# Attention with 1024-column steps, two exponentials a step, row maxima laid down by DMA, and the output's two parts added by a transfer in the projection

## The reference: what is computed

```python
ada = silu(c) @ W_ada + b_ada
h = _modulate(_layernorm(x), shift_msa, scale_msa)
qkv = (h @ W_qkv + b_qkv).reshape(b, l, 3, H, D)      # H = 16 heads of D = 36, l = 1024
scores = einsum('blhd,bmhd->bhlm', q * D ** -0.5, k)
attn = softmax(scores, axis=-1)
o = einsum('bhlm,bmhd->blhd', attn, v).reshape(b, l, c)
x = x + gate_msa * (o @ W_proj + b_proj)
# then an MLP of width 4 * 576 with its gate, and x + (z @ R - z) @ U^T
```

## Time and profile before

| | us |
|---|---|
| device time, median of 3 (3438.27 to 3440.93) | 3439.12 |
| span of the profiled execution, first to last instruction | 3409.0 |
| time outside the span (the difference) | 30.1 |
| attention, first score tile to last store | 760 to 2013 |
| projection, its stage | 2015 to about 2305 |
| busy in the span: TensorE, VectorE, ScalarE, GpSimd | 2925.1, 1807.5, 1467.3, 1632.2 |

### The profile page before, as it was taken

How to read it: one execution, slowest core, us unless ns; L and a number is a source line. 1 busy time by engine, 2 the same in 40 slices (tenths; PEclk the granted TensorE clock), 3 DMA queues, 4 the chain that set the end, 5 groups by cost and what they waited for, 6 DMA issues and landing times. The chain is left out here.

```text
span 3409.0 us, 53673 instructions
## 1 busy us (share of the span) xinstructions
PE 2925.1 (86%) x16130; PEld 2355.6 (69%) x16130; DVE 1807.5 (53%) x3056; ACT 1467.3 (43%) x2832; POOL 1632.2 (48%) x1401
## 2 busy tenths in 40 slices
PE   6759889968888898888889867757999999999976
PEld 2247677745656665665656536656999999999975
DVE  3445465447888888888888857770111111111125
ACT  2122222217888888888888852221111111111112
POOL 1232222116888888888888866781222222222210
PEclk9769899978999999999999978878999999999989
DMA  5379999983323332333323234659211112121144
GB/s 175 118 239 178 182 226 187 167 170 67 67 67 74 67 75 64 73 68 69 71 65 77 64 105 168 238 180 326 67 34 59 42 34 67 34 67 34 42 118 161
DMA packets 457636, 373.83 MB, mean 110 GB/s; under 512 B 293649, under 2 KB 357785, under 8 KB 457486
## 3 DMA queue, kind: packets, MB, share of 16 engines
q1 hardware_dynamic: 450008, 359.12, 42.1%
q10 hardware_dynamic: 7482, 12.69, 1.2%
HBM read 221.81 MB, written 149.36 MB: 109 GB/s over the span
## 5 line engine op out<-in xcount | busy, mean ns | idle before, releaser
L755 POOL TENSOR_TENSOR a_pl<-a_pf,a_ph 128x512 fp32r<-128x512 f32 x768 | 1040.3, 1386 | 215.7 <-ACT a_ph L830 215.2
L770 DVE TENSOR_REDUCE a_mx<-a_psum_s 128x1 f32<-128x1024 f32 x512 | 618.7, 1219 | 178.6 <-PE a_psum_s L861 173.9
L830 ACT ACTIVATE a_ph<-a_pf 128x512 fp32r<-128x512 f32 x1024 | 673.1, 657 | 0.0
L825 ACT ACTIVATE a_pf<-a_psum_t 128x512 f32<-128x512 f32 x1024 | 634.6, 620 | 57.0 <-PE a_psum_t L878 54.3
L1434 POOL TENSOR_TENSOR m_al<-m_af,m_ah 128x256 fp32r<-128x256 f32 x288 | 213.0, 740 | 767.9 <-DVE m_ah L1443 767.9
L1482 PE MATMUL m_psum_h<-m_ht,m_w 128*128 128x256 f32 x4032 | 534.1, 284 | 34.9 <-DMA m_w<-w_s 24.4
L1482 PEld LDWEIGHTS m_psum_h<-m_ht,m_w 128*128 128x128 f32 x4032 | 508.4, 189 | 38.3 <-issue 37.0
L1443 DVE CAST m_ah<-m_af 128x256 fp32r<-128x256 f32 x288 | 84.5, 293 | 840.6 <-ACT m_af L1420 840.6
L1496 PE MATMUL m_psum_y<-m_w,m_ah 128*128 128x288 f32 x2304 | 505.9, 296 | 1.4 <-DVE m_y L1460 1.2
L1420 ACT ACTIVATE m_af<-m_psum_h,m_bias 128x256 f32<-128x256 f32 x288 | 137.0, 476 | 817.9 <-PE m_psum_h L1482 817.9
L893 PE MATMUL a_psum_o<-a_ph,a_vs 128*100 128x512 f32 x1024 | 438.2, 428 | 32.5 <-DVE a_pl L803 25.6
(11 more groups left out here) (218 smaller groups left out, 3111.0 us busy)
## 6 DMA issues: line engine op xcount, KB each, us to landing
a_qs<-q_s SPq DMA_DIRECT2D x192, 144.0 KB
a_ks<-k_s SPq DMA_DIRECT2D x192, 144.0 KB
w_s<-q_ws SPq DMA_DIRECT2D x64, 324.0 KB, 3.8
h_s<-p_ht SPq DMA_DIRECT2D x40, 512.0 KB, 5.1
m_ht<-h_s SPq DMA_DIRECT2D x16, 1280.0 KB, 8.4
v_s<-q_vo SPq DMA_DIRECT2D x64, 288.0 KB, 8.7
a_vs<-v_s SPq DMA_DIRECT2D x128, 144.0 KB
q_s<-q_qko SPq DMA_DIRECT2D x32, 512.0 KB, 3.7
```

Source lines behind the costliest of these rows:

```text
L755: pool.tensor_tensor(pl[:, s % RING], pf[:, s % RING], raw(ph[:, s % RING]), ALU.subtract).then_inc(lo_pool, 1)
L770: dve.tensor_reduce(mx[:, u % 2, t:t + 1], p_s[:, bank(u, t)], AX.X, ALU.max) \
L825: act.activation(pf[:, s % RING], p_t[:, s % 2], ACT.Exp, scale=SCALE) \
L830: act.activation(ph[:, s % RING], pf[:, s % RING], ACT.Copy).then_inc(hi_ready, 1)
```

## The change

In the attention a step has 128 keys twice (`PAIR`), so 8 steps of 1024 columns a head; scores run 2 steps ahead. ScalarE takes the exponential twice from PSUM, once rounded to `ph` and once in full. On steps 0 and 4 (`DVE_LO`) the full one is written over the scores in PSUM, and VectorE subtracts from there; on the other six it goes to `pf`, and GpSimd subtracts. `p_t` now needs four PSUM banks, so `p_s` is a single buffer. A score tile takes every eighth query (`t:L:KT`), so that partition c of `mx` holds the maxima of 8 neighbouring queries; VectorE splits `mx` itself in two operations of 8 columns (`split_max`), and the DMA lays them down as a row. Transpose, `turn_hi` and the identity are gone. `finish` only copies 100 rows; both parts go to `o_t`, and in the projection GpSimd adds the second part onto `ot` by accumulating DMAs (`add_low`), for which `operand` waits.

```diff
-    STEPS = LH * KT
-    AHEAD = 5
+    PAIR = 2
+    STEPS = LH * KT // PAIR
+    AHEAD = 2
+    LO_AHEAD = 2
-    dve_lo = lambda s: s % 4 == 3
+    DVE_LO = (0, 4)
-        p_s = ps("s", [P, 2, L])
-        p_t = ps("t", [P, 2, GT])
+        p_s = ps("s", [P, L])
+        p_t = ps("t", [P, 2, COLS])
...
+                def split_max(hd, u, puts):
+                    if puts is not None:
+                        dve.wait_ge(max_in[(u + 2) % SLOTS], START + 32 * puts)
+                    dve.wait_ge(s_free, KT * (hd + 1))
+                    dve.tensor_scalar(mh[:, u % 2, 0], mx[:, u % 2], -1.0, None, ALU.mult).then_inc(mh_hi, 1)
+                    dve.wait_ge(mh_hi, hd + 1)
+                    dve.scalar_tensor_tensor(mh[:, u % 2, 1], mx[:, u % 2], -1.0, raw(mh[:, u % 2, 0]),
+                                             ALU.mult, ALU.subtract).then_inc(mh_lo, 1)
+                def low(hd, s):
+                    dve.wait_ge(exp_done, STEPS * hd + s + 1)
+                    dve.tensor_tensor(pl[:, s % RING], p_t[:, s % 2], raw(ph[:, s % RING]), ALU.subtract) \
+                       .then_inc(lo_dve, 1)
+                def finish(hd, lh):
+                    dve.wait_ge(p_free, RING + STEPS * hd + PER_LH * (lh + 1))
+                    dve.wait_ge(o_out[lh], START + 16 * STORES * hd)
+                    dve.tensor_copy(ob[:, lh], p_o[0:VW, lh]).then_inc(o_copied[lh], 1)
...
+                    for s in range(STEPS):
+                        if not (last and u >= SLOTS - 2):
+                            max_tile(hd + 2, (u + 2) % SLOTS, s)
+                        if s == 0 and not (last and u == SLOTS - 1):
+                            split_max(hd + 1, (u + 1) % SLOTS, i if u == 0 else i + 1)
+                        if s + LO_AHEAD in DVE_LO:
+                            low(hd, s + LO_AHEAD)
+                        if s + LO_AHEAD - STEPS in DVE_LO and not (last and u == SLOTS - 1):
+                            low(hd + 1, s + LO_AHEAD - STEPS)
+                        if (s + 1) % PER_LH == 0:
+                            finish(hd, s // PER_LH)
...
+                        act.wait_ge(t_ready, STEPS * hd + s + 1)
+                        act.wait_ge(p_free, STEPS * hd + s + 1)
+                        act.activation(ph[:, s % RING], p_t[:, s % 2], ACT.Exp, scale=SCALE)
+                        full = p_t[:, s % 2] if s in DVE_LO else pf[:, s % RING]
+                        act.activation(full, p_t[:, s % 2], ACT.Exp, scale=SCALE).then_inc(exp_done, 1)
...
+                def score_tile(hd, u, i, t):
+                    if t == 0:
+                        pe.wait_ge(loaded[u], 16 * LOADS * (i + 1))
+                    if not (isinstance(hd, int) and hd == 0 and t == 0):
+                        pe.wait_ge(s_free, KT * hd + t)
+                    for h in range(L // 512):
+                        m = pe.matmul(p_s[:, h * 512:(h + 1) * 512], qs[0:SROWS, u, t:L:KT],
+                                      ks[0:SROWS, u, h * 512:(h + 1) * 512], start=True, stop=True)
+                    m.then_inc(s_ready, 1)
+                def scores(hd, u, i, s):
+                    if s >= 2 and s - 2 in DVE_LO:
+                        pe.wait_ge(lo_dve, lo_counts(hd, s - 2)[1])
+                    elif not (isinstance(hd, int) and hd == 0 and s < 2):
+                        pe.wait_ge(exp_done, STEPS * hd + s - 1)
...
+                def add_low(g, b, half):
+                    cols = slice(half * GT, (half + 1) * GT)
+                    pool.wait_ge(o_in, 64 * (g + 1))
+                    pool.dma_start(ot[:, 0:FULL], o_t[1, bass.ds(b * C, FULL * P), cols]
+                                   .rearrange("(k p) n -> p k n", p=P), accum_op=ALU.add).then_inc(o_sum, 16)
+                    for r in range(2):
+                        pool.dma_start(ot[r * REM:(r + 1) * REM, FULL], o_t[1, bass.ds(b * C + FULL * P, REM), cols],
+                                       accum_op=ALU.add).then_inc(o_sum, 16)
...
                     i.then_inc(xn_ready, 1)
+                    if more == 2:
+                        add_low(g + 2, b + 1, half)
...
                     dve.wait_ge(r_ready, NK * g + c + 1)
+                    if c == 0:
+                        dve.wait_ge(o_sum, 48 * (g + 1))
```

More of the change, by code:

```diff
@@ L685, in heads @@
                 body(SLOTS * (n - 1) + u, u, n - 1, True)
[L687 to L693, removed]
         def lo_counts(n_heads, s):
-            d = sum(dve_lo(x) for x in range(s + 1))
+            d = sum(x <= s for x in DVE_LO)
             return NPOOL * n_heads + s + 1 - d, NDVE * n_heads + d
@@ L725, in _, with store @@
                 put_max(0, 0)
+                def store(hd, lh):
+                    cols = slice(lh * GT, (lh + 1) * GT)
+                    sp.wait_ge(o_copied[lh], START + hd + 1)
+                    for s, r in enumerate((0, VLO)):
+                        sp.dma_start(o_t[s, bass.ds(hd * D, D), cols], ob[r:r + D, lh]).then_inc(o_out[lh], 16)
+                    sp.dma_start(sums[bass.ds(hd, 1), cols], ob[ONES:ONES + 1, lh]).then_inc(o_out[lh], 16)
                 def body(hd, u, i, last):
+                    if not (last and u == SLOTS - 1):
+                        put_max(hd + 1, (u + 1) % SLOTS)
                     if not (last and u > 0):
@@ L791, in _ @@
                     if hd == 0:
[L792 removed]
+                        split_max(0, 0, None)
+                for s in DVE_LO:
+                    if s < LO_AHEAD:
+                        low(0, s)
                 def body(hd, u, i, last):
                     for s in range(STEPS):
[L796 to L799, removed]
[L800 to L807 removed]
+                        if not (last and u >= SLOTS - 2):
[8 more added lines that the diff above has]
+                            finish(hd, s // PER_LH)
                 heads(nc.vector, body)
@@ L882, in values @@
+                    for r in range(PAIR):
+                        t = PAIR * j + r
+                        m = pe.matmul(p_t[:, s % 2, r * GT:(r + 1) * GT], ks[0:MROWS, u, t * P:(t + 1) * P],
+                                      qs[0:MROWS, u, lh * GT:(lh + 1) * GT], start=True, stop=True)
+                    m.then_inc(t_ready, 1)
                 def values(hd, u, s):
-                    lh, t = divmod(s, KT)
-                    if t == 0:
+                    lh, j = divmod(s, PER_LH)
@@ L891, in values @@
                         pe.wait_ge(lo_pool, n_pool)
-                    out = p_o[0:VW, lh]
-                    pe.matmul(out, vs[:, u, t], ph[:, s % RING], start=(t == 0), stop=False)
-                    m = pe.matmul(out, vs[:, u, t], pl[:, s % RING], start=False, stop=(t == KT - 1))
+                    for r in range(PAIR):
+                        t = PAIR * j + r
+                        cols = slice(r * GT, (r + 1) * GT)
+                        pe.matmul(p_o[0:VW, lh], vs[:, u, t], ph[:, s % RING, cols], start=(t == 0), stop=False)
+                        m = pe.matmul(p_o[0:VW, lh], vs[:, u, t], pl[:, s % RING, cols], start=False,
+                                      stop=(t == KT - 1))
                     m.then_inc(p_free, 1)
```

137 lines of the change are left out of this document (33 added, 104 removed).

## The result

The changed kernel takes 3699.18 us (median of 4, 3694.79 to 3702.94), the kernel before 3438.69 us beside it: 1.077 times as long, 95% interval 1.075 to 1.079. The forecast was 3735 us, range 3515 to 3830.

What follows compares the result with a forecast made beforehand. Near-equal ScalarE, TensorE and GpSimd ceilings, plus waits at the maxima's turn and VectorE and GpSimd shutting each other out. Attention 214, start 17, projection 65 take the span from 3409.0 to 3705; with 30.1, 3735 us, range 3515 to 3830.

Steps and rivals of the forecast that it cites:

- The head: One head of the attention: 22.5 us forecast against 19.15 before, +214 us over 64 heads.
- ring: Attention, step 2's exponentials to step 6's through GpSimd's low, values, score tile, reduction, low(4), scores: two make 18.6 us a head.
- delay: Both split_max operations on VectorE wait out GpSimd subtractions, so low(4) starts 2.9 us later: 21.5 us a head.
- clock: TensorE's clock falls after 2.7 us idle once a head: 1.0 us a head taken, bounds 0 to 27.
- The rival that only one operation waits: One of split_max's two waits, or they fall in a GpSimd gap: head 19.0 to 19.4 us, 3525 us, chance 0.17.
- Only the ring: Rival: neither split_max operation waits for GpSimd; 18.8 us a head, 3500 us, chance 0.07.
- The start: First score tiles: with one p_s, matmul and reduction alternate, 16 tiles take 41 us against 23.5: +17 us.
- Strided weights: Score tile's weight loads with a step of 8 elements: taken as 0, at most +150 us.
- The projection: Operand 0 waits for GpSimd's accumulating DMAs, 8 to 13 us later a group: +65 us, bounds +30 and +110.
- The 30.1 us that I called outside the span: Gap between the kernel before's median, 3439.1 us, and its profiled span, 3409.0, added to the forecast span of 3705.
- ceiling, 16.3 us: Head time in the attention towards which the head falls if the ring does not bind: -182 us.
- the rival that the head gets faster: Attention: the ring does not bind, hops and the 1024-column subtraction being shorter than priced: 3340 us, chance 0.07.

Runs made afterwards that it cites:

- e1: The changed kernel with the split of the maxima taken off VectorE, as three 8-column operations on GpSimd ahead of its step 3 subtraction: 3515.59 us.
- e6: The changed kernel with six matmuls of zeros a head on TensorE, ahead of the score tile of step 2: 3659.05 us.
- e2: The changed kernel with TensorE issuing a step's score tile ahead of that step's value matmuls: 3530.38 us.
- e3: The changed kernel with the output part undone: finish has its second operation back, no accumulating transfers in the projection: 3643.46 us.
- e4: The changed kernel with a score tile taking 128 neighbouring queries, so weight loads are contiguous (only the time is read): 3687.61 us.
- e9: The kernel before with the output part alone: finish copies 100 rows, GpSimd adds the second part in the projection: 3396.81 us, ratio 0.986.

## Why the prediction was right

**The head.** Forecast 22.5 us, measured 22.02. Mechanism as predicted: both operations wait out GpSimd (1.88 and 2.29 us), the score tile waits 2.3 us (forecast 2.7), the clock falls. Taken off in the order e1, e6 the terms are: ring 18.97 (forecast 18.6), delay 21.32 - 18.97 = 2.35 (forecast 2.9), clock 22.02 - 21.32 = 0.70 (forecast 1.0). Too little in the ring, too much in the other two, and the errors cancel in part; that much of the closeness is luck. The price of 1273 ns for 512 columns on GpSimd stands in none of the rows that the prediction names; it is the median of line 1110, a subtraction of the same shape in the projection. The 2.35 us made from it measured 2.39.

**The addition of ring and delay** is the step that the runs correct. I treated the delay as an amount laid on a fixed ring. e2 opens the ring, leaves the split where it is, and gets to 19.27; e1 removes the split, leaves the ring, and gets to 18.97; both together (with e3) give 18.64. Each needs the other to cost 3 us; the delay itself shrank from 4.2 to 2.5 us in e2, and in both runs the clock is at 1.00, which e6 prices at 0.70. The sum came out right for the combination that was built, and would have been wrong for either part taken away: by it e2 should have stayed near 22.

**The rival that only one operation waits** is out in the changed kernel (1880 and 2290 ns). In e2 it nearly comes about (0.70 and 1.80 us on average). "Only the ring" gave 18.8 a head and 3500 us; e1, which is that case, has 18.97 and 3516.

**The start.** Forecast +17; first score tile at 780.9, first exponential at 821.5, 40.6 us for 23.5: +17.1.

**Strided weights.** Taken as 0, bounds 0 to 150; e4 says 12 us in time, 26 by the head.

**The projection.** Forecast +65, measured +66. Operand 0 is 11.6 us later a group in the mean (8 to 13 forecast), the accumulating transfer lands in 10.4 us (5.5 to 11 forecast). The sum closes in another way than it was made: the groups are 41.0 us apart for 32.2, so that 8.8 of the 11.6 count, 53 in six groups (60 forecast), and the start costs 13 (operand 0 comes 14.7 us behind the first spread matmul, for 1.3), where 5 was forecast.

**The sum.** Attention 231 forecast and 201 measured, projection 65 and 66. The mis-sized term is the head's: (22.5 - 19.15) x 64 = 214 was forecast, and (22.02 - 19.12) x 64 = 186 measured. The 30.1 us that I called outside the span was misnamed: after the change the time is the span plus 1.6 us, and the timed runs of the kernel before are 1.6 to 1.8 us above their spans too. The profiled execution of before was itself ahead of its timed runs; its attention starts at 760.2, that of every other profile at 777.0 to 797.0, with the same code in front. Adding the 30.1 to the sum was still the right correction.

**What the removed operation is worth.** I let `finish`'s second operation enter only as VectorE's load, and so at nothing. In the changed kernel that holds (e3, head unmoved); in the kernel before it was worth 1.8 us a head (e9). The prediction of the whole didn't depend on it, but a forecast for the parts of this change would have: the part that I priced as pure loss is the one that pays.

**What stays open:** why the stages ahead of the attention move by up to 20 us between programs whose code there is the same (medians a few us apart are no evidence here), how e9's gain divides, and what the last 18 us of the projection are. The prediction's "ceiling, 16.3 us" in the rival that the head gets faster has no working; the largest of its own ceilings is TensorE's 15.0.

## What to carry to other kernels

Judge a change's parts each in both surroundings: the output part costs 56 us in the changed attention and gives 46 in the old one. Its 1.4 us of VectorE are worth nothing in the one head (22.02 either way) and 1.8 us in the other. On VectorE an operation of 8 columns can cost as much as the GpSimd operation that it meets; put it on GpSimd itself, or shorten what it meets. Where TensorE stands idle once a period, look at the spacing of the matmuls behind the gap, not only at the gap.

## What the runs showed of the hardware that was not expected

An operation with one SBUF source, 128 x 8, waited out GpSimd's 2.36 us subtraction as one with two sources did (1880 ns median, 170 alone), and one that asked 0.13 us before GpSimd's operation ended got in between two that ran back to back. Six matmuls of zeros a head made the kernel 40 us faster. A weight load with a step of 8 fp32 elements took 324 ns, contiguous 189. An accumulating transfer of 1 MB landed in 10.4 us, a plain one in 5.3, and its issue held GpSimd 1.22 us. Twice an addition of VectorE with both sources in SBUF (line 1134, 128 x 576) took 8.9 us beside GpSimd's issues of these transfers and the four operations behind them; its median is 0.93.
